# The second feed-forward product in float32, straight from the gelu's output

## What is computed

```
si = x @ attn_w[l, :d];  sj = x @ attn_w[l, d:]
scores = si[:, :, None] + sj[:, None, :] + attn_b[l]
attn = softmax(where(mask, leaky_relu(scores), -inf))
agg = einsum('bij,bjd->bid', attn, x)
h = layernorm(x + agg, g1[l], beta1[l])
ff = gelu(h @ W1[l] + b1[l]) @ W2[l] + b2[l]      # 256 -> 1024 -> 256
x = layernorm(h + ff, g2[l], beta2[l])
```

## Time and profile before

| | us |
|---|---|
| median of 3 runs | 2702.7 (2700.8 to 2707.65) |
| the profiled execution | 2699.2 |
| its span, first to last instruction | 2697.5 |
| PE busy | 2357.2 (87%) |
| DVE busy | 1833.0 (68%) |
| ACT busy | 1566.6 (58%) |
| POOL busy | 1286.5 (48%) |

### The profile page before, as it was taken

One profiled execution on the slowest core, in us unless ns is written; L12 is line 12 of the kernel. 1 busy time (PEld: TensorE's weight loads), 2 busy tenths in 40 slices (PEclk: granted clock), 3 DMA queues, 4 the chain that ended last, 5 costly groups with the idle time before them and its releaser, 6 DMA issues.

```text
span 2697.5 us, 41567 instructions
## 1 busy us (share of the span) xinstructions
PE 2357.2 (87%) x14721; PEld 1760.6 (65%) x14721; DVE 1833.0 (68%) x4906; ACT 1566.6 (58%) x2423; POOL 1286.5 (48%) x2212
## 2 busy tenths in 40 slices
PE   3889999878899989899798988999888999999868
PEld 2566666646676666676576766677665677667656
DVE  7677677437677667776677766868657576666655
ACT  4457666445566555565556665665636556656544
POOL 5555465523365434644356542655434555446411
PEclk9999999989899999999899998999989999999988
DMA  4312021101120112110211102111121010100000
GB/s 175 123 40 86 5 86 40 52 4 40 59 87 5 40 43 91 52 36 9 73 61 55 36 13 74 56 52 36 38 92 40 24 36 9 36 9 21 23 12 30
DMA packets 66051, 128.15 MB, mean 48 GB/s; under 512 B 12956, under 2 KB 53172, under 8 KB 62772
## 3 DMA queue, kind: packets, MB, share of 16 engines
q1 hardware_dynamic: 65844, 125.50, 14.0%
HBM read 110.80 MB, written 14.68 MB: 47 GB/s over the span
## 4 chain that ended last, share of the span: by engine, by line
PE 57%; DVE 21%; ACT 8%; POOL 6%; issue 6%; DMA 1%; SPq 0%; DVEq 0%; POOLq 0%; ACTq 0%
PE OB L1413 35%; PE FB L1413 13%; DVE mj L1063 5%; PE RB L1413 4%; DVE pw L1086 4%; ACT nms L780 3%; DVE junk L1003 2%; PE TH L1413 2%; DMA adjst<-in_x 1%; DVE st L952 1%; DVE junk L1008 1%; POOL xc L541 1%; DVE xc L979 1%; ACT xc L725 1%; ACT gT L759 1%
## 5 line engine op out<-in xcount | busy, mean ns | idle before, releaser
L1413 PE MATMUL OB<-xx,pw 128*128 128x257 f32 x4096 | 980.4, 398 | 26.0 <-DVE xc L979 16.7
L1413 PEld LDWEIGHTS OB<-xx,pw 128*128 128x128 f32 x4096 | 798.3, 199 | 168.7 <-DVE xc L979 21.1
L1413 PE MATMUL FB<-hT,wb 128*128 128x512 f16 x2304 | 564.1, 383 | 67.6 <-DVE gT L1100 42.0
L1413 PE MATMUL OB<-wb,gT 128*128 128x256 f16 x4608 | 575.2, 273 | 4.3 <-POOL gT L554 4.2
L1413 PEld LDWEIGHTS OB<-wb,gT 128*128 128x128 f16 x4608 | 449.8, 98 | 137.5 <-POOL gT L554 8.1
L554 POOL TENSOR_TENSOR gT<-g,gT 128x512 f16<-128x512 f32 x192 | 229.2, 1194 | 612.7 <-ACT gT L759 612.3
L725 ACT ACTIVATE xc<-xc,nb,rs 128x256 f32<-128x256 f32 x384 | 212.8, 589 | 375.3 <-POOL nb L529 375.2
L1086 DVE SCALAR_TENSOR_TENSOR pw<-r2s,sj,RB 128x512 f32<-128x512 f32 x512 | 365.4, 740 | 77.6 <-PE RB L1413 74.7
L1413 PEld LDWEIGHTS FB<-hT,wb 128*128 128x128 f16 x2304 | 212.9, 98 | 276.7 <-DVE gT L1100 49.1
L541 POOL TENSOR_TENSOR xc<-xc,gb 128x256 f32<-128x256 f32 x384 | 289.9, 755 | 94.0 <-ACT xc L725 94.0
L765 ACT ACTIVATE pw<-pw,sj 128x512 f32<-128x512 f32 x512 | 327.7, 708 | 8.6 <-DVE pw L1086 8.3
(11 more groups left out here) (112 smaller groups left out, 2565.6 us busy)
## 6 DMA issues: line engine op xcount, KB each, us to landing
wb<-w_scratch SPq DMA_DIRECT2D x19, 2048.0 KB, 7.8
adjst<-in_adj SPq DMA_DIRECT2D x56, 512.0 KB, 4.2
xx<-in_x SPq DMA_DIRECT2D x16, 512.0 KB, 5.5
nm<-in_L_gnn_W SPq DMA_DIRECT2D x6, 1024.0 KB, 9.4
gb<-in_L_gnn_g SPq DMA_DIRECT2D x48, 128.0 KB, 2.8
gb<-in_L_gnn_beta SPq DMA_DIRECT2D x48, 128.0 KB, 3.4
adjst<-in_x SPq DMA_DIRECT2D x6, 1024.0 KB, 6.8
out_x<-adjst SPq DMA_DIRECT2D x48, 128.0 KB, 1.7
```

Source lines behind the costliest of these rows:

```text
L1413: return pe.matmul(o, lhsT, rhs, start=first, stop=last)
```

## The change

The gelu's output goes in float32 straight into a ring, `gF`, which is the old `gT` seen as float32. Its 16-bit copy on ACT and both subtractions (DVE's and POOL's) are gone, and so are `g32` and three semaphores. W2 is kept as float32, scaled, in `w2f`, and `wb` holds only the halves of W1. `second` has one float32 matmul of 256 columns where it had three of 16 bits. PE waits for the gelu alone. The load of the other layer's weights is two DMAs of half the size, and in the first two steps the passes that made W2's halves become one.

```diff
@@ second(k, n), PE
                     if b == 0:
-                        pe.wait_ge(*glo(i))
-                    w2h, w2l = wb[:, 2, f * D:(f + 1) * D], wb[:, 3, f * D:(f + 1) * D]
+                        pe.wait_ge(gelu_done, i + 1)
                     for c in range(2):
...
-                        gh, gl = gT[:, i % GRING, 0, rows], gT[:, i % GRING, 1, rows]
-                        mm(o, gh, w2h, False, False)
-                        mm(o, gh, w2l, False, False)
-                        ins = mm(o, gl, w2h, False, f == FT - 1 and c == 1)
+                        ins = mm(o, gF[:, i % GRING, rows], w2f[:, f * D:(f + 1) * D], False, f == FT - 1 and c == 1)
@@ hidden(k, n), PE
                 if i >= 2:
-                    if i % 2 == 0:
-                        pe.wait_ge(glo_even, i // 2)
-                    else:
-                        pe.wait_ge(gelu_done, i - 1)
+                    pe.wait_ge(gelu_done, i - 1)
@@ gelu(k, n), ACT
-                src = FB[i % 2][:, :]
-                if n % 2 == 1:
-                    if i >= 2:
-                        act.wait_ge(glo_odd, i // 2)
-                    dst = g32[:, :]
-                else:
-                    dst = src
-                act.activation(dst, src, ACT.Gelu, bias=b1c[:, layer(k), f:f + 1], scale=1.0 / W_SCALE)\
-                   .then_inc(gelu_done, 1)
-                act.wait_ge(gelu_done, i + 1)
                 if i >= GRING:
                     act.wait_ge(*second_done(i - GRING))
-                act.activation(gT[:, i % GRING, 0, :], dst, ACT.Copy).then_inc(ghi_done, 1)
+                act.activation(gF[:, i % GRING, :], FB[i % 2][:, :], ACT.Gelu, bias=b1c[:, layer(k), f:f + 1],
+                               scale=1.0 / W_SCALE).then_inc(gelu_done, 1)
@@ g_low(k, n), POOL (odd rounds)
-                pool.wait_ge(ghi_done, i + 1)
-                pool.tensor_tensor(out=gT[:, i % GRING, 1, :], in0=g32[:, :], in1=gT[:, i % GRING, 0, :],
-                                   op=ALU.subtract).then_inc(glo_odd, 1)
@@ g_low(k, n), DVE (even rounds)
-                dve.wait_ge(ghi_done, i + 1)
-                dve.tensor_tensor(out=gT[:, i % GRING, 1, :], in0=FB[i % 2][:, :], in1=gT[:, i % GRING, 0, :],
-                                  op=ALU.subtract).then_inc(glo_even, 1)
@@ step(k), SP
                             sp.dma_start(wb[:, :, :].rearrange("p a b -> p (a b)"), w_scratch[ln])\
                                 .then_inc(w_ready, 16)
+                            sp.dma_start(w2f[:, :], w2_scratch[ln]).then_inc(w_ready, 16)
```

More of the change, by code:

```diff
@@ L138, in build @@
     adj_v = adj.rearrange("b (t p) n -> b p t n", p=P)
-    w_scratch = nc.dram_tensor("w_scratch", (LAYERS, P, 4 * 2048), f16).ap()
+    w_scratch = nc.dram_tensor("w_scratch", (LAYERS, P, 2 * 2048), f16).ap()
+    w2_scratch = nc.dram_tensor("w2_scratch", (LAYERS, P, 2048), f32).ap()
     ctx = ExitStack()
@@ L157, in build @@
         xc = sb("xc", [P, 2, NT, D])
-        wb = sb("wb", [P, 4, 2048], f16)
+        wb = sb("wb", [P, 2, 2048], f16)
+        w2f = sb("w2f", [P, 2048])
         hT = sb("hT", [P, 2, KD, N], f16)
         gT = sb("gT", [P, GRING, 2, HALF], f16)
-        g32 = sb("g32", [P, HALF])
         r2s = sb("r2s", [P, N])
@@ L213, in build @@
         csum6 = b2r[:, :, :].rearrange("p l d -> p (l d)")[:, 0:2 * D].bitcast(f32)
+        gF = gT[:, :, :, :].rearrange("p r a n -> p r (a n)").bitcast(f32)
         adj0 = pw[:, :, :].rearrange("p t n -> p (t n)").bitcast(i32).rearrange("p (t n) -> p t n", t=NT)
@@ L272, in build @@
         gelu_done = sem("gelu_done")
-        ghi_done = sem("ghi_done")
         exp_done = sem("exp_done")
@@ L290, in build @@
         htl_done = sem("htl_done")
-        glo_even = sem("glo_even")
         max_done = sem("max_done")
@@ L393, in store_piece @@
                 sp.wait_ge(piece_lo, i + 1)
-                sp.dma_start(w_scratch[l][:, m * 4096:(m + 1) * 4096], nm2[:, 4096:8192].bitcast(f16))\
-                    .then_inc(w_stored, 16)
+                if m == 0:
+                    sp.dma_start(w_scratch[l], nm2[:, 4096:8192].bitcast(f16)).then_inc(w_stored, 16)
+                else:
+                    sp.dma_start(w2_scratch[l], nm2[:, 4096:8192].bitcast(f32)).then_inc(w_stored, 16)
             def start():
@@ L458, in step @@
                     sp.dma_start(w_scratch[0], wb[:, :, :].rearrange("p a b -> p (a b)")).then_inc(w0_stored, 16)
+                    sp.dma_start(w2_scratch[0], w2f[:, :]).then_inc(w0_stored, 16)
                 if k < 2:
@@ L473, in step @@
                         if layer(k) != ln:
-                            sp.wait_ge(w0_stored, 16)
+                            sp.wait_ge(w0_stored, 32)
                             if ln > 0 and later[0] == STEP_OF[(0, ln)]:
@@ L802, in piece_high @@
                     act.wait_ge(w_stored, 16 * i)
-                act.activation(nm2[:, 4096:6144].bitcast(f16), nm2[:, 0:4096].bitcast(f32), ACT.Copy,
-                               scale=W_SCALE).then_inc(piece_hi, 1)
+                raw = nm2[:, 0:4096].bitcast(f32)
+                if i % 2 == 0:
+                    act.activation(nm2[:, 4096:6144].bitcast(f16), raw, ACT.Copy, scale=W_SCALE).then_inc(piece_hi, 1)
+                else:
+                    act.activation(nm2[:, 4096:8192].bitcast(f32), raw, ACT.Copy, scale=W_SCALE).then_inc(piece_lo, 1)
             def opening(k):
@@ L927, in _ @@
             r2_copy(0)
[L928 to L931, removed]
+            act.wait_ge(w0_ready, 32)
+            act.activation(wb[:, 0, :], nm2.bitcast(f32)[:, 0:2048], ACT.Copy, scale=W_SCALE).then_inc(w0_hi, 1)
+            act.activation(w2f[:, :], nm2.bitcast(f32)[:, 2048:4096], ACT.Copy, scale=W_SCALE).then_inc(w0_lo, 1)
             for it in range(NT):
@@ L1175, in piece_low @@
             def piece_low(i):
-                dve.wait_ge(piece_hi, i + 1)
+                dve.wait_ge(piece_hi, i // 2 + 1)
                 dve.scalar_tensor_tensor(out=nm2[:, 6144:8192].bitcast(f16), in0=nm2[:, 0:4096].bitcast(f32),
@@ L1253, in ffn_step @@
                         edges(raw, t)
-                    if k == 0 and t in (1, 3):
+                    if k == 0 and t == 1:
                         w0_low(t // 2)
@@ L1272, in ffn_step @@
                         ht_low(k, 3)
-                    if k < 2 and n in (5, 12):
-                        piece_low(2 * k + n // 12)
+                    if k < 2 and n == 5:
+                        piece_low(2 * k)
                     if n == 8:
@@ L1448, in hidden @@
                     elif weight_loads(k) > 0:
-                        pe.wait_ge(w_ready, 16 * weight_loads(k))
+                        pe.wait_ge(w_ready, 32 * weight_loads(k))
                 if f == 0:
```

11 lines of the change are left out of this document (removed).

## The result

The changed kernel takes 2750.5 us (median of 4 runs, 2749.4 to 2756.8) where the kernel before takes 2701.8 beside it: +48.7 us, ratio 1.0181, 95% interval 1.0159 to 1.0203. The forecast was slower, with 2806 and a range from 2765 to 2860: the direction was right, the size more than twice too large, and the time lies where the third rival put it (2754). The profiled execution of the changed kernel took 2756.75 us, 6 above its median; its span is 2754.9, +57.4 on the one before. What follows compares the two profiled executions where it reads traces, and medians where it compares times.

What follows compares the result with a forecast made beforehand. PE was taken to bound the kernel, busy 94% of the rounds, no other engine near its limit. +187 for float32 less 82 of waits and work gave +105: 2804 profiled, 2806 as median, range 2765 to 2860.

Steps and rivals of the forecast that it cites:

- the third rival: All idle time near the rounds goes: 136 us come back, +51, 2754 us; chance 0.09.
- The price, +187: `second` on PE takes 1.79 us instead of 1.31, entry into float32 included: 0.48 us more in each of 384 rounds.
- What it takes away, -82: Waits and work that vanish in and behind the rounds and in the first steps: 33 + 4 + 18 + 18 + 6 + 3.
- (c): Other PE idle time in the rounds, mostly waits for DVE: half of 36 us goes as DVE is freed, -18.
- (d): Behind each stretch of rounds DVE is on time for `residual2`: -18 of 41.6 us of PE idle time.
- (a): At each stretch's start `hidden(2)` no longer waits for DVE's subtraction, only for the gelu: -33 of 42.0 us.
- (b): `second` no longer waits for POOL's subtraction: -4 us.
- (e): PE's granted clock may not fall after shorter stalls, in three or four of five stretches: -6 us.
- (f): In the first two steps three of DVE's six large weight passes go: -3 us, a guess.
- The first: The stalls stay, as waits are handed on to the gelu and `residual2`: +147, 2850 us; chance 0.12.
- The second: Each float32 group's entry and exit is dear in a mixed stream: 65 us more, +170, 2872 us; chance 0.08.
- The fourth and fifth: Gelu, copy, subtraction pace the rounds: 2700 or less, 0.02; float32 matmul is one full-price record, not two: 2530, 0.01.

Runs made afterwards that it cites:

- units-between: The changed kernel with the groups of 128-column bf16 score matmuls moved between `hidden` and `second`: 2758.4 us, +53.6 on the kernel before.
- longer rounds: The kernel before with only the product of the gelu's low half made twice, 16 instead of 12 16-bit matmuls a round: 2814.8 us, +110.0.
- price alone: The changed kernel with the old copies, subtractions and waits put back beside the float32 product: 2800.9 us, +96.0 on the kernel before.

## Why the prediction was wrong

The forecast was +105 and the profiled executions have +57. All of this lies in PE's busy time. Its idle time was forecast to fall by 76 us (33 + 4 + 18 + 18 + 3) and fell by 76. Its busy time was to rise by 187 - 6 = 181 and rose by 133. Two terms failed: the price of the product, 28 us too high, and the busy time of PE's other matmuls, which was to fall by 6 us with the clock and fell by 26. That the idle time comes out to the microsecond is luck: it did not go by the steps that were given for it.

*What bounds the kernel* was half right. PE's idle time in the rounds was small, and the float32 product did set the sign. But "no engine but PE is near its limit" was read from sums over whole stretches. In parts of them PE keeps running into engines that are behind: 160 to 167 us more work took 32 to 39 us of idle time away, and 167 less brought 27.

*The price, +187: mis-sized by 28 us.* It is 159 by the groups and 0.41 to 0.42 us a round. The failed step is "I take the column sum's price, because its neighbours are full 128-row matmuls as in a round". The neighbour that counts is the one ahead, and its width: in 14 of 16 rounds `second` stands right behind `hidden` with its 512 columns, as the earlier trace rows show. The units-between run shows both prices in one kernel's groups. Nor does the bias matmul, 512 columns wide, bring a second entry. The lower bound of the forecast, 8 x 0.216, was right. The estimate from the Trainium skill ("FP8 and Floating Point Precision", section "TensorE Precision Notes", 4 passes for 3) was 168 and came nearer than the row that I chose; the traces agree with its count, 1.72 / 1.31 = 1.31 for 4/3.

*What it takes away, -82: 20 us too small and wrongly shared out.* By place, the sum in the rounds was 33 + 4 + 18 + 6 = 61 and is 159 - 88 = 71, of which 57 are idle time (forecast 55) and 14 busy time (forecast 6); behind them 18 and is 25; in the rest 3 and is 5. So 28 + 10 + 7 + 2 = 47 us are the difference between +105 and the +57 of the profiled executions, and 48.7 by medians comes with 6 and 3 us that the two profiled executions lie off theirs.

By cause it is another account, from medians: of 160 us of price 64 are absorbed by the longer rounds alone (price alone, +96), 16 by the waits for the subtractions, 31 by the freed engines, which leaves +49. PE's idle time went by 39, 14 and 23 us in these three steps. The forecast had nothing for the first of them but a part of (c) and (d).

- (a), the wait at the start, -33, was the largest term and the worst reasoned. Its mechanism happened, the waits for the subtraction went and those for the gelu are 8.0 us, as forecast near 9. But a wait that is removed is worth its length only if the engines waited for can keep up afterwards. Alone it gave nothing (+6.0): the wait came again two rounds on, and the clock fell in nine more stretches. In longer rounds it gave 22.
- (b) and the gelu's new wait for the ring: as forecast, the product waits for nothing.
- (c) and (d) were right in place and close in size (idle time 25 and 18 us left, forecast 27 and 24). Their cause was given as freed DVE time; the larger part comes from the longer rounds alone, which already bring 82 and 41.6 us to 60 and 25.
- (e) was right where it was looked for: four stretches rose to PEclk 1.00 and three are left under it. The stretch of this kind that had run at 1.00 before has PE busy 1.4 us less than the earlier trace rows (58.41 against 59.83), 6 us for four. It was too narrow: PE's busy time other than the product fell by 14 us in the rounds, 2 behind them and 9 in the rest, 26 in all, where the forecast had 6. The group of the aggregates, which no edit touches, went from 980.4 to 969.5 us, and the mean granted clock of the span from 0.951 to 0.957 up to 0.963 to 0.967. How much of the other 20 us is the clock stays open.
- (f): the span outside rounds and their ends is 4.9 us shorter. What of this is the weights' preparation was not tried; PE's busy time in the aggregates is a part of it, and it scatters in the other runs too (-15 with the price alone).
- The split DMA never showed in a wait.

*The rivals.* The first ("the stalls stay", 2850) was built as if stalls could stay while rounds grow: with every old wait in place the kernel takes 2801. The third, which I gave 0.09, has the right time, but not for its reason: 43 us of idle time are still there in and behind the rounds, and half of its distance from my forecast is the price, the other half busy time of PE's other matmuls. The second had a surcharge for each entry; there is none after `hidden`. The fourth and fifth fall by the price: PE paid 0.41 us a round, and the float32 product has 3072 records of full price.

## What to carry to other kernels

Work added to the busiest engine can cost less than its length, and work removed give less, when other engines catch up or fall behind meanwhile: here 0.6 to 0.7 of it arrived either way, even at 94% busy in the stretch. Do not put all of the difference down to waits. Compare the busy time of the instructions that were not changed as well: here it made a third to nearly half of what did not arrive. A wait shown at the start of a stretch has no known worth until one knows that the engine waited for would not be late again at the next place; shorten it in a copy of the kernel and look where the waits go. And where a dearer form removes work from engines that are behind, try it in the rounds where they are, and not in all: two blocks of eight made this kernel 0.8% faster, all eight made it 1.8% slower.

## What was not expected of the hardware

A float32 matmul group of 256 columns pays 0.06 us on entry after 128-column bf16 matmuls and nothing after 512-column ones, f16 or bf16. Its weight loads last 0.190 us each (the groups above), longer than the 0.055 us at which narrow matmuls go by (0.22 us for the four from 246.18 to 246.40) and shorter than the 0.216 of wide ones; that the load sticks out there is an argument from these numbers and was not tried by itself. And the granted clock answered to small edits: shortening one wait raised the stretches with PEclk under 1.00 from 7 to 12 of 24, and in the rounds of the profiled run PE was busy 17 us longer for the same matmuls, more than the 6 us of idle time that had been saved there. In the step shown above the clock fell after PE had stood still for 1.99 us where it had stood for 1.35 and 0.36. Why it fell in other stretches is open: the stretch from 1787.70 in the kernel before, which stays at 1.00, holds a stall of 2.85 us as well.
